# Six of layer 1's forty attention units multiplied as three f16 products instead of one f32 product

## The chip, the core and the metric

One core of a Trainium2 chip runs the whole layer as one program. The metric is the device time of one execution in microseconds (us). The numbers of the kernel before are the median of three timed runs and one profiled execution. The engines in the profile are PE (TensorE matmuls; PEld is its weight loads), DVE (VectorE), ACT (ScalarE), POOL (GpSimd) and SP (SyncE), which here only issues DMAs.

## The reference

The layer takes 1250 nodes with 768 features and 41,250 edges. It adds three things to the nodes: a graph network with two attention layers, a linear attention, and a mixture of 8 experts. The change lies in the first attention layer of the graph network, which has 4 heads of 192 features:

```
h = (x @ W).reshape(n, H, C)
s_src = (h * a_src).sum(-1)
s_dst = (h * a_dst).sum(-1)
e = jax.nn.leaky_relu(s_src[src] + s_dst[dst], NEG_SLOPE)
emax = jax.ops.segment_max(e, dst, num_segments=n)
ee = jnp.exp(e - emax[dst])
denom = jax.ops.segment_sum(ee, dst, num_segments=n)
alpha = ee / denom[dst]
out = jax.ops.segment_sum(alpha[:, :, None] * h[src], dst, num_segments=n)
```

## The kernel before, in words

The kernel does no gather over edges. An early stage counts the edges into a dense table `CT` of 1250 x 1250 (source tiles of 128 nodes on the partitions). Attention is then dense: for one head `h` and one source tile `t` the weights are a matrix of 128 sources by 1250 targets, and the sum over sources is a matmul. One such pair (`h`, `t`) is a **unit**. Layer 1 has 4 heads x 10 tiles = 40 units, unit `10h + t`, in that order on every engine. A unit passes four steps:

- `slopes` (DVE, L1611): the logits before the exponential, 128 x 1250 f32, from two rows that a DMA copied to all partitions.
- `expo` (ACT, L1189): the exponential, in place.
- `weights` (DVE, L1617): clip and multiply by the edge counts. The result goes to one of three buffers `PT1[unit % 3]`. From unit 3 on it waits until PE has finished unit - 3 (`s_agg`).
- `aggregate` (PE, L2323): ten matmuls, one for each tile of 128 targets. The stationary operand is a 128 x 128 slice of `PT1`, the moving one 193 columns of `G4` (192 features of the head and a column of ones, whose sum is the denominator). They add up in PSUM over the ten units of a head.

DVE's program order in layer 1 is, in iteration i: `slopes(i)`, `weights(i-1)`; in a head's iteration t = 2 also `denominators` of the head before (L1729, waits until PE has finished that head's last unit), and in t = 5 `head_added` (L1736: adds the scaled head to the sum `h2x`). ACT does `expo(i)` and in t = 2, 3, 4 scales the ten result tiles of the head before out of PSUM (`head_scaled`, L1201). PE's unit 10h cannot write its fourth pair of target tiles before ACT has scaled the first pair of the head before.

The features `G` are made some 200 us earlier, in a stage called the G stage here: PE makes `x @ M` for node tile t, ACT scales it out of PSUM to `GBUF` (L1131), DVE reads the two logit columns from it (`logits_out`, L1552), SP stores it to memory (`g_d`, L748). They come back just before layer 1, in three DMAs of tiles 0-1, 2-4 and 5-9. After each of the three, POOL writes the column of ones (L933, L939, L941) and PE waits for that with `s_sel_ready` (9, 10 and 11) in units 0-1, 2-4 and 5-9 of head 0. On SP the third of these DMAs is followed by two stores of rows that are needed later (`xl_d`, L831, semaphore `late_rows`), by the load of the mask, and by the loads of three expert units `held` (L827) into arena memory that is free in layer 1; the expert loads wait for `late_rows`.

Of the kernel before, what the change touches and what calls it, by code (L numbers as in the profile page):

```python
# [5 lines left out]
ALU = mybir.AluOpType  # L6
ACT = mybir.ActivationFunctionType
# [16 lines left out]
def gps_layer(nc, x, src, dst, norm_g, norm_b, W1, a_src1, a_dst1, b1, W2, a_src2, a_dst2, b2, Wu, bu,  # L24
# [27 lines left out]
    with ctx:  # L52
# [22 lines left out]
        def reg(off, words, rows=P):  # L75
            return arena[0:rows, off:off + words]
# [114 lines left out]
        EARLY = 3  # L191
        assert EARLY * NP <= 4608

        def slope_buf(unit):
            return early[:, unit, :] if unit < EARLY else BUF[:, unit % 3, :]

# [134 lines left out]
        rr_d = nc.dram_tensor("rr_d", (H1 * 2 * NT * P,), F32, kind="Internal").ap()  # L331
        fr_d = nc.dram_tensor("fr_d", (2 * NE, P, 2, UNIT), F16, kind="Internal").ap()

        held = range(0, 3)
        graphed = range(3, 5)
        masked = range(6, 9)
        summed = (5, 9, 10, 11)
        freed = (14,)
        late = (12, 13, 15)
        assert sorted([*held, *graphed, *masked, *summed, *freed, *late]) == list(range(2 * NE))  # L340
        NCONV = 2 * NE * NPIECE

        def piece(c):
# [211 lines left out]
        sums_out = (s_sum0_out, s_sum1_out)  # L555
        brows_in = (s_brow0_in, s_brow1_in)
        z_in = rows_back + brows_in
        assert NT % 2 == 0
        XAS = 8 * NT
        masks_in = (s_mask0_in, s_mask1_in)  # L560
# [78 lines left out]
        def _(sp):  # L639
# [105 lines left out]
            conv_in(NKV + 2)  # L745
            for t in range(NT):
                sp.wait_ge(s_g_copied, t + 1)
                sp.dma_start(g_d[:, t * GW:(t + 1) * GW], GBUF[:, t % 3, :]).then_inc(gbufs[t % 3], 16)  # L748
                if t:
                    convs(conv_of_g[t - 1])  # L750
                if t == 1:
                    sp.wait_ge(s_kvsum_ready, 1)
                    sp.dma_start(brow, bu.partition_broadcast(P)).then_inc(s_bias_in, 16)
                if t == 8:
                    sp.wait_ge(s_stage_low, 3 * CUTS)
                    weight(3, Wu[0:D, :])
# [83 lines left out]
                rr_load(h)  # L840
            sp.wait_ge(s_agg, agg_done(H1 * NT))
            sp.dma_start(LXT.rearrange("p b r k n -> p (b r k n)"), xl_d.bitcast(F16)).then_inc(late_rows, 16)
            sp.wait_ge(s_head_out, 5 * H1)
            sp.wait_ge(s_late_psum, 2 * len(LATER))
            for u in graphed:
# [26 lines left out]
        def _(pool):  # L872
# [56 lines left out]
            for r in (0, 2 * KC, 4 * KC):  # L929
                select(g.affine_select(out=rows_of, in_=rows_of, compare_op=ALU.not_equal, fill=1.0, base=-r,  # L930
                                       pattern=[[-2, KC], [-1, 2], [0, 64]], channel_multiplier=1))
            pool.wait_ge(s_gbuf0, 80)
            select(g.memset(G4[:, 0:2, :, CW], 1.0))  # L933
# [5 lines left out]
            select(g.memset(G4[:, 2:5, :, CW], 1.0))  # L939
            pool.wait_ge(s_gbuf2, 64)  # L940
            select(g.memset(G4[:, 5:NT, :, CW], 1.0))  # L941

            fmade = [0]

# [81 lines left out]
        def _(act):  # L1026
# [97 lines left out]
            for t in range(NT):  # L1124
                act.wait_ge(s_g_psum, t + 1)
                if t >= 3:
                    act.wait_ge(gbufs[t % 3], 16 * (t // 3))
                    act.wait_ge(s_g_ready, t - 2)
                for c in range(2):
                    h = slice(c * 2 * HW, (c + 1) * 2 * HW)  # L1130
                    i = a.activation(GBUF[:, t % 3, h], ps[2 * (t % 2) + c][:, 0:2 * HW], ACT.Identity, scale=rs[:, 3, t:t + 1])  # L1131
# [72 lines left out]

            SCALED = {2: range(0, 4), 3: range(4, 7), 4: range(7, NT)}

            def out_high(n):
                h, a0, a1 = OUT2[n]
                act.wait_ge(s_o2t_psum, 4 + n + 1)
                a.activation(out2T[0:KS, 0, h, a0:a1], PS[0:KS, 2 * 512 + a0:2 * 512 + a1], ACT.Identity, bias=b2c[:, h:h + 1]).then_inc(s_o2t_ready, 1)  # L1210
# [116 lines left out]
        def _(dve):  # L1327
# [220 lines left out]

            def logits_out(t):
                dve.wait_ge(s_g_copied, t + 1)  # L1550
                logits = GBUF[:, t % 3, :].rearrange("p (h n) -> p h n", h=H1)[:, :, CW:CW + 2]
                V.tensor_tensor(ASD[:, :, :, t].rearrange("p r h -> p h r"), logits, bm, ALU.add).then_inc(s_g_ready, 1)  # L1552

            for t in range(NT):
                if t:
                    edges(KV_STEPS + 2 * t)
                    edges(KV_STEPS + 2 * t + 1)
                    logits_out(t - 1)
# [53 lines left out]

            def weights(unit, i, t, deep):
                dve.wait_ge(s_e_ready, unit + 1)
                if i >= deep:
                    dve.wait_ge(s_agg, agg_done(unit + 1 - deep))
                V.scalar_tensor_tensor((PT1 if deep == 3 else PT)[i % deep][:, 0:N], z_of(unit), 2.0, CT[:, t, 0:N], ALU.min, ALU.mult).then_inc(s_p_ready, 1)  # L1617

            dve.wait_ge(s_kvwo_psum, KC)
            for d in range(2):  # L1620
# [135 lines left out]
            def layer1():  # L1756
                for i in range(H1 * NT):
                    h, t = divmod(i, NT)
                    if t == 0 and h:
                        dve.wait_ge(rr_in[h % 2], 16 * (h // 2 + 1))  # L1760
                    if i >= EARLY:
                        slopes(i, h, t)
                    if i >= 2:
                        weights(i - 1, i - 1, (i - 1) % NT, 3)
                    if t == 2 and h:
                        denominators(h - 1)
                    if t == 5 and h:
# [275 lines left out]
        def _(pe):  # L2043
# [152 lines left out]
            for t in range(NT):  # L2196
                if t >= 2:
                    pe.wait_ge(s_g_copied, t - 1)
                for c in range(2):
                    m = product(ps[2 * (t % 2) + c][:, 0:2 * HW], xnt(t * P, (t + 1) * P), cols(MG, c * 2 * HW, (c + 1) * 2 * HW))  # L2200
                    if c:
                        m.then_inc(s_g_psum, 1)
                    edges(KV_STEPS + 2 * t + c)
                if t == 2:
                    pe.wait_ge(s_kvsum_ready, 1)
                    for j in range(KC):
                        m = T.transpose(ps[6 + j // 3][:, (j % 3) * P:(j % 3 + 1) * P], bd[:, j, :], ident[:, :])
# [64 lines left out]
            for n, (c0, w) in enumerate(CH):  # L2272
# [31 lines left out]
                for t in range(t + 2, (c0 + w) // P):  # L2304
# [27 lines left out]
            for i in range(H1 * NT):  # L2332
                h, t = divmod(i, NT)
                if i == NT:
                    pe.wait_ge(s_acc_ready, NT)
                if i < NT:
                    pe.wait_ge(s_sel_ready, 9 if t < 2 else 10 if t < 5 else 11)
                aggregate(i, i, t, h, CW, 3, G4[:, t, h, 0:CW + 1])

            def keep_warm(n, bank):  # L2340
                for _ in range(n):
# [254 lines left out]
```

## Time and profile before

| | us |
|---|---|
| median of 3 runs (lowest, highest) | 963.11 (962.73, 963.61) |
| the profiled execution: its own time | 964.2 |
| its span in the trace | 962.4 |
| PE busy over the span | 912.5 (95%) |
| DVE busy over the span | 746.1 (78%) |
| ACT busy over the span | 350.1 (36%) |
| POOL busy over the span | 134.2 (14%) |

1.8 us of the profiled execution lie outside its span. A row of a timeline gives start and duration of a run of equal instructions; the durations of neighbours overlap, since the next instruction starts before the last one has drained. So the cost of one instruction in a stream is the distance from start to start, called its **pitch** below, and not its duration. An f32 matmul shows as two records, so that a unit of ten matmuls is 20 records. A note in brackets at the end of a row is idle time ahead of it and what ended it.

### The profile page before, as it was taken

How to read it: one execution, taken by the hardware profiler on the slowest of the kernel's cores; microseconds unless marked ns; L12 is line 12 of the kernel's file. 1: busy time of each engine (PE TensorE's matmuls, PEld its weight loads, DVE VectorE, ACT ScalarE, POOL GpSimd, SP SyncE). 2: the span in 40 equal slices, each digit the busy share in tenths (PEclk: the TensorE clock that was granted, in tenths of full speed). 3: DMA queues.
4: the chain of work that ended last, by engine and by line, in shares of the span. 5: the costliest groups of instructions: out<-in, count | busy, mean ns of one | idle time of the engine just before them, and what ended most of it. 6: DMA issues, size and time to landing. Idle time of an engine off the chain costs nothing.

```text
span 962.4 us, 17237 instructions
## 1 busy us (share of the span) xinstructions
PE 912.5 (95%) x6379; PEld 670.4 (70%) x6381; DVE 746.1 (78%) x1704; ACT 350.1 (36%) x464; POOL 134.2 (14%) x153
## 2 busy tenths in 40 slices
PE   6899999989999999999999999989997899999995
PEld 5667676756665555567799999679866666666662
DVE  7878999997877799895889997889989544444443
ACT  5751212122235314314345552465446223232320
POOL 3400000000002000000000000020010344545441
PEclk9999999999999999999999999999998899999998
DMA  9610212246367689697792000189475668778860
GB/s 324 193 60 24 77 62 70 72 172 236 116 215 226 215 270 267 186 285 259 246 390 83 12 1 1 34 196 330 167 283 216 258 162 196 185 183 195 201 156 3
DMA packets 78844, 164.29 MB, mean 171 GB/s; under 512 B 28308, under 2 KB 47638, under 8 KB 75818
## 3 DMA queue, kind: packets, MB, share of 16 engines
q1 hardware_dynamic: 63402, 117.18, 35.9%
q0 software_dynamic: 10944, 38.22, 16.5%
q10 hardware_dynamic: 4416, 7.78, 2.2%
q8 instruction: 54, 0.88, 0.4%
q14 instruction: 28, 0.23, 0.1%
HBM read 109.13 MB, written 50.51 MB: 166 GB/s over the span
## 4 chain that ended last, share of the span: by engine, by line
PE 72%; DVE 18%; DMA 3%; issue 3%; ACT 2%; SPq 1%; DVEq 1%; ACTq 0%; POOLq 0%; POOL 0%
PE PS L2050 46%; PE PS L2323 15%; PE PS L2151 3%; DVE arena L1784 3%; PE PS L2521 2%; DVE arena L1611 1%; DVE arena L1432 1%; DVE arena L1617 1%; DMA arena<-in_L_ffn_W_dram 1%; PE PS L2162 1%; PE PS L2536 1%; PE PS L2342 1%; DVE arena L1594 1%; DVE arena L1497 1%; PE PS L2219 1%
## 5 line engine op out<-in xcount | busy, mean ns | idle before, releaser
L2050 PE MATMUL PS<-arena 128*128 128x384 f16 (+7 forms) x3396 | 561.5, 321 | 7.8 <-DVE arena L2040 3.0
L2050 PEld LDWEIGHTS PS<-arena 128*128 128x128 f16 (+2 forms) x3396 | 319.9, 99 | 214.3 <-issue 10.0
L2323 PE MATMUL PS<-arena 128*128 128x193 f32 (+1 forms) x1200 | 178.4, 310 | 3.2 <-DVE arena L1617 2.5
L2323 PEld LDWEIGHTS PS<-arena 128*128 128x128 f32 x1200 | 176.4, 191 | 5.3 <-DVE arena L1617 3.8
L1189 ACT ACTIVATE arena<-arena,AS 128x1250 f32<-128x1250 f32 x60 | 79.9, 1338 | 74.7 <-DVE arena L1611 74.6
L1617 DVE SCALAR_TENSOR_TENSOR arena<-arena 128x1250 f32<-128x1250 f32 x60 | 87.1, 1453 | 5.8 <-PE PS L2323 5.7
L1497 DVE TENSOR_SCALAR arena<-arena 128x240 f16<-128x240 f16 x324 | 88.8, 274 | 0.0
L1611 DVE SCALAR_TENSOR_TENSOR arena<-arena,AS 128x1250 f32<-128x1250 f32 x55 | 83.0, 1508 | 0.0
L1496 DVE TENSOR_SCALAR arena<-arena 128x128 f16<-128x128 f16 x324 | 79.8, 246 | 0.1
L2039 DVE SCALAR_TENSOR_TENSOR arena<-PS,arena 128x768 f32<-128x768 f32 x27 | 25.8, 957 | 62.6 <-PE PS L2050 62.6
L1321 ACT ACTIVATE arena<-PS 128x1536 f16<-128x1536 f16 x27 | 39.1, 1449 | 74.8 <-PE PS L2521 74.8
L1594 DVE CUSTOM_DVE_ANT_0 arena<-arena 128x1250 bf16<-128x1250 f32 x40 | 58.3, 1457 | 0.8
L1004 POOL DMA_INDIRECT out_dram<-arena x27 | 43.3, 1602 | 87.8 <-DVE arena L2040 58.0
L1070 ACT ACTIVATE arena<-arena 128x768 f16<-128x768 f32 x48 | 39.8, 838 | 32.0 <-DMA arena<-in_L_ffn_W_dram 32.0
L1437 DVE SCALAR_TENSOR_TENSOR arena<-arena 128x768 f16<-128x768 f32 x48 | 45.9, 966 | 4.1 <-ACT arena L1070 3.8
L1489 DVE TENSOR_TENSOR arena<-arena,PS 128x240 f32 x81 | 32.3, 399 | 19.0 <-PE PS L2151 14.4
L1099 ACT ACTIVATE arena<-arena 128x768 f32<-128x768 f32 x10 | 8.3, 843 | 100.1 <-DVE arena L1446 100.1
L2151 PE MATMUL PS<-arena 128*128 128x240 f16 x324 | 42.4, 266 | 2.5 <-DVE arena L1489 2.5
L2017 DVE SCALAR_TENSOR_TENSOR arena<-PS,arena 128x384 f32<-128x384 f32 x27 | 15.0, 557 | 37.9 <-PE PS L2050 36.1
L2151 PEld LDWEIGHTS PS<-arena 128*128 128x128 f16 x324 | 31.4, 98 | 11.2 <-DVE arena L1497 3.1
L1315 ACT ACTIVATE arena<-arena 128x384 f32<-128x384 f32 x27 | 14.1, 522 | 68.6 <-DVE arena L2017 68.6
L987 POOL DMA_INDIRECT arena<-xf_d,arena x27 | 26.0, 963 | 62.7 <-DVE arena L1992 54.7
(276 smaller groups left out, 914.0 us busy)
## 6 DMA issues: line engine op xcount, KB each, us to landing
arena<-in_L_ffn_W_dram SPq DMA_DIRECT2D x48, 384.0 KB, 3.8
fr_d<-arena SPq DMA_DIRECT2D x48, 384.0 KB, 3.3
arena<-fr_d SPq DMA_DIRECT2D x16, 1152.0 KB, 12.3
arena<-in_x_dram SPq DMA_DIRECT2D x18, 384.0 KB, 5.6
arena<-rr_d SPq DMA_DIRECT2D x4, 1280.0 KB, 8.6
g_d<-arena SPq DMA_DIRECT2D x10, 388.0 KB, 2.4
acc_d<-arena SPq DMA_DIRECT2D x10, 384.0 KB, 3.4
xf_d<-arena ACTq DMA_DIRECT2D x10, 384.0 KB, 3.5
```

The costliest lines, as they stand in the source:

```text
L1004: g.indirect_dma_start(out=out, out_offset=bass.IndirectOffsetOnAxis(ap=found[:, i:i + 1].bitcast(U32), axis=0), in_=Yb[:, i % 2, :], in_o ...
L1070: a.activation(cbuf[b][:, PIECE:PIECE + PIECE // 2].bitcast(F16), cbuf[b][:, 0:PIECE], ACT.Copy, scale=UP).then_inc(s_conv_high, 1)
L1189: a.activation(z, z, ACT.Exp, bias=AS2[:, h, t:t + 1]).then_inc(s_e_ready, 1)
L1437: V.scalar_tensor_tensor(buf[:, 0:PIECE // 2].bitcast(F16), buf[:, 0:PIECE], UP, buf[:, PIECE:PIECE + PIECE // 2].bitcast(F16), ALU.mult, ...
L1496: V.tensor_scalar(ohlo[:, u % OB, j, :], iota[:, 0:P], kc[:, 1, j, u:u + 1], None, ALU.is_equal)
L1497: i = V.tensor_scalar(ohk[:, u % OB, j, :], iota[:, 0:NT * W], kc[:, 0, j, u:u + 1], None, ALU.is_equal)
L1594: V.tensor_tensor_reduce(out=junk1[:, 0:N], in0=arow1[h][:, 0:N], in1=mask1[d % 2].rearrange("p t d -> p (t d)")[:, 0:N], scale=1.0, scala ...
L1611: V.scalar_tensor_tensor(z_of(unit), RR[:, h % 2, 0, 0:N], AS8[:, h, t:t + 1], RR[:, h % 2, 1, 0:N], ALU.add, ALU.max).then_inc(s_t2_ready, 1)
L1617: V.scalar_tensor_tensor((PT1 if deep == 3 else PT)[i % deep][:, 0:N], z_of(unit), 2.0, CT[:, t, 0:N], ALU.min, ALU.mult).then_inc(s_p_rea ...
L2050: m = T.matmul(out, left[i][x], right[i][y], start=first and i + r == 0, stop=last and 3 * i + r == n - 1)
L2151: i = T.matmul(ps[4 + u % 2][:, 0:NT * W], ohlo[:, u % OB, j, :], ohk[:, u % OB, j, :], start=j == 0, stop=j == EJ - 1)
L2323: m = T.matmul(ps[sum_bank(h, b)][:, r * (C + 1):(r + 1) * (C + 1)], (PT1 if deep == 3 else PT)[i % deep][:, d * P:(d + 1) * P], feats, st ...
```

## The change

The units of `SPLIT` = 8, 13, 18, 23, 28, 33 (tiles 3 and 8 only) are multiplied in another form. Their weights and their features are each held as an f16 high part and an f16 low part (the rest). Then high x high, high x low and low x high are added: 30 f16 matmuls stand where 10 f32 matmuls stood. For that

- ACT makes the high part of the weights (`weights_high`) and DVE the low part (`weights_low`), into a ring of two pairs in the arena memory where expert unit 2 was held; that unit's load moves behind layer 1 (`paired`);
- in the G stage, tiles 3 and 8 are written in parts: ACT writes the high part, DVE the low part (`logits_out`), SP and PE wait for DVE there;
- POOL writes the column of ones head by head for these tiles (1 in the high part, 0 in the low part), and also pads the pairs' columns 1250 to 1279, for which it waits for `late_rows`;
- `weights` of unit u + 3 waits for `weights_low(u)` where it waited for PE's unit u.

```diff
+        SPLIT = (8, 13, 18, 23, 28, 33)
+        SPLIT_TILES = sorted({u % NT for u in SPLIT})
+        pairs = reg(2 * UNIT, 2 * NP).bitcast(F16).rearrange("p (b r n) -> p b r n", b=2, r=2)
...
+        def runs(t, c):
+            h = 2 * c
+            kinds = [k * NT + t in SPLIT for k in (h, h + 1)]
+            return [(h, h + 2, kinds[0])] if kinds[0] == kinds[1] else [(h, h + 1, kinds[0]), (h + 1, h + 2, kinds[1])]
...
-        held = range(0, 3)
+        held = range(0, 2)
+        paired = (2,)
...
             for t in range(NT):
                 sp.wait_ge(s_g_copied, t + 1)
+                if t in SPLIT_TILES:
+                    sp.wait_ge(s_g_ready, t + 1)
                 sp.dma_start(g_d[:, t * GW:(t + 1) * GW], GBUF[:, t % 3, :]).then_inc(gbufs[t % 3], 16)
...
+            for u in paired:
+                experts(u)
...
+            def ones_column(a, b):
+                for t in range(a, b):
+                    for c in range(2):
+                        for h0, h1, split in runs(t, c):
+                            if split:
+                                g.memset(g_pair(G[:, t, :], h0, h1)[:, :, 1, CW], 0.0)
+                                i = g.memset(g_pair(G[:, t, :], h0, h1)[:, :, 0, CW], 1.0)
+                            else:
+                                i = g.memset(G4[:, t, h0:h1, CW], 1.0)
+                return i
...
             pool.wait_ge(s_gbuf2, 64)
-            select(g.memset(G4[:, 5:NT, :, CW], 1.0))
+            pool.wait_ge(late_rows, MASKS + 32)
+            for b in range(2):
+                g.memset(pairs[:, b, 0, N:NP], 1.0)
+                g.memset(pairs[:, b, 1, N:NP], 0.0)
+            select(ones_column(5, NT))
...
+            def weights_high(unit):
+                k = SPLIT.index(unit)
+                if k == 0:
+                    act.wait_ge(s_acc_psum, NT)
+                    act.wait_ge(late_rows, MASKS + 32)
+                if k >= 2:
+                    act.wait_ge(s_agg, agg_done(SPLIT[k - 2] + 1))
+                act.wait_ge(s_p_ready, unit + 1)
+                a.activation(pairs[:, k % 2, 0, 0:N], PT1[unit % 3][:, 0:N], ACT.Copy).then_inc(split_high, 1)
...
                     expo(i, h, t)
+                    if i - 1 in SPLIT:
+                        weights_high(i - 1)
...
             def logits_out(t):
                 dve.wait_ge(s_g_copied, t + 1)
+                if t in SPLIT_TILES:
+                    for c in range(2):
+                        for h0, h1, split in runs(t, c):
+                            if split:
+                                made = v3(ps[2 * (t % 2) + c][:, (h0 - 2 * c) * HW:(h1 - 2 * c) * HW], h1 - h0)
+                                row = g_pair(GBUF[:, t % 3, :], h0, h1)
+                                V.scalar_tensor_tensor(row[:, :, 1, :], made, rs[:, 3, t:t + 1], row[:, :, 0, :], ALU.mult, ALU.subtract)
+                        made = v3(ps[2 * (t % 2) + c][:, 0:2 * HW], 2)[:, :, CW:CW + 2]
+                        i = V.scalar_tensor_tensor(ASD[:, :, 2 * c:2 * c + 2, t].rearrange("p r h -> p h r"), made, rs[:, 3, t:t + 1],
+                                                   bm[:, 2 * c:2 * c + 2, :], ALU.mult, ALU.add)
+                    i.then_inc(s_g_ready, 1)
+                    return
...
             def weights(unit, i, t, deep):
                 dve.wait_ge(s_e_ready, unit + 1)
-                if i >= deep:
+                if unit - 3 in SPLIT:
+                    dve.wait_ge(split_low, NK + SPLIT.index(unit - 3) + 1)
+                elif i >= deep:
                     dve.wait_ge(s_agg, agg_done(unit + 1 - deep))
...
+            def weights_low(unit):
+                k = SPLIT.index(unit)
+                dve.wait_ge(split_high, NK + k + 1)
+                V.tensor_tensor(pairs[:, k % 2, 1, 0:N], PT1[unit % 3][:, 0:N], pairs[:, k % 2, 0, 0:N], ALU.subtract).then_inc(split_low, 1)
...
                     if i >= 2:
                         weights(i - 1, i - 1, (i - 1) % NT, 3)
+                    if i - 2 in SPLIT:
+                        weights_low(i - 2)
...
+            def aggregate_pairs(unit, t, h):
+                k = SPLIT.index(unit)
+                pe.wait_ge(split_low, NK + k + 1)
+                row = g_pair(G[:, t, :], h, h + 1)
+                for d in range(NT):
+                    b, r = divmod(d, 2)
+                    for x, y in ((0, 0), (0, 1), (1, 0)):
+                        m = T.matmul(ps[sum_bank(h, b)][:, r * (CW + 1):(r + 1) * (CW + 1)], pairs[:, k % 2, x, d * P:(d + 1) * P], row[:, 0, y, 0:CW + 1],
+                                     start=False, stop=False, skip_group_check=True)
+                m.then_inc(s_agg, 1)
```

Two places in the engines' programs show what the diff alone doesn't. The first is POOL just ahead of layer 1, where it writes the ones that PE waits for; `gbuf0` to `gbuf2` are the three DMAs that bring the features back, and `mask0_out` is the semaphore of `late_rows`. Before:

```order
L933 MEMSET arena 128x8 [waits gbuf0,sel_ready]
L936 MEMSET arena 128x30 [waits acc_psum,sel_ready]
L936 MEMSET arena 128x30 x2
L939 MEMSET arena 128x12 [waits gbuf1,sel_ready]
L941 MEMSET arena 128x20 [waits gbuf2,sel_ready]
```

And after, from `gbuf2` on (between `gbuf1` and `gbuf2` there are 9 memsets in place of one):

```order
L974 MEMSET arena 128x30 [waits mask0_out,gbuf2,sel_ready]
L975 MEMSET arena 128x30
L974 MEMSET arena 128x30
L975 MEMSET arena 128x30
L960 MEMSET arena 128x2 x6
L957 MEMSET arena 128x2
L958 MEMSET arena 128x2
L957 MEMSET arena 128x1
L958 MEMSET arena 128x1
L960 MEMSET arena 128x1
L960 MEMSET arena 128x2 x2
```

In place of one memset behind the third DMA there stand 17 behind that DMA and `late_rows`, and only the last of them lets PE start unit 5.

The second place is DVE in head 1, from the wait for head 0's last unit on (L1803 is `denominators`, L1678 `slopes`, L1686 `weights`, L1691 `weights_low`, L1810 `head_added`; `w1t_ready` and `w1t_psum` are the semaphores that the high and the low part use). After:

```order
L1803 RECIPROCAL rden<-PS 128x10 [waits agg]
L1678 SCALAR_TENSOR_TENSOR arena<-arena,AS8 128x1250 [waits p_ready]
L1686 SCALAR_TENSOR_TENSOR arena<-arena 128x1250 [waits agg,e_ready]
L1678 SCALAR_TENSOR_TENSOR arena<-arena,AS8 128x1250 [waits p_ready]
L1686 SCALAR_TENSOR_TENSOR arena<-arena 128x1250 [waits agg,e_ready]
L1678 SCALAR_TENSOR_TENSOR arena<-arena,AS8 128x1250 [waits p_ready]
L1686 SCALAR_TENSOR_TENSOR arena<-arena 128x1250 [waits agg,e_ready]
L1691 TENSOR_TENSOR arena<-arena 128x1250 [waits w1t_ready]
L1810 TENSOR_TENSOR arena<-arena 128x16x96 [waits head_out]
L1810 TENSOR_TENSOR arena<-arena 128x4x96
L1678 SCALAR_TENSOR_TENSOR arena<-arena,AS8 128x1250 [waits p_ready]
L1686 SCALAR_TENSOR_TENSOR arena<-arena 128x1250 [waits w1t_psum,e_ready]
```

Between the wait for head 0's last unit and the low part of unit 13 stand three pairs of `slopes` and `weights`, and `head_added` follows it directly. Before, the same rows stood there without the L1691 row.

## Rows read from the trace of the kernel before

**Rows 1.** Groups of instructions by line, 471 to 603 us, shapes apart.

```profile
L2323 PE MATMUL PS<-arena 128*128 128x193 f32 x800 | 130.9, 327 | 0.6 <-POOL arena L936 0.6
L1611 DVE SCALAR_TENSOR_TENSOR arena<-arena,AS 128x1250 f32<-128x1250 f32 x38 | 57.3, 1508 | 0.0
L1617 DVE SCALAR_TENSOR_TENSOR arena<-arena 128x1250 f32<-128x1250 f32 x39 | 56.7, 1453 | 2.6 <-PE PS L2323 2.5
L1189 ACT ACTIVATE arena<-arena,AS 128x1250 f32<-128x1250 f32 x38 | 50.9, 1339 | 53.9 <-DVE arena L1611 53.8
```

**Rows 2.** Timeline of PE, the start and the end of layer 1.

```profile
471.51 28.66 PE L2323 MATMUL PS<-arena 128*128 128x193 f32 x174 [0.61 <-POOL arena L936]
...
479.75 122.66 PE L2323 MATMUL PS<-arena 128*128 128x193 f32 x750
602.25 0.82 PE L2358 MATMUL PS<-ident,arena 128*96 128x128 f32 x6
```

**Rows 3.** Timeline of DVE at the change from head 0 to head 1.

```profile
504.45 0.22 DVE L1729 RECIPROCAL rden<-PS 128x10 f32<-128x10 f32 x1 [1.74 <-PE PS L2323]
...
507.34 1.51 DVE L1611 SCALAR_TENSOR_TENSOR arena<-arena,AS 128x1250 f32<-128x1250 f32 x1
508.77 1.45 DVE L1617 SCALAR_TENSOR_TENSOR arena<-arena 128x1250 f32<-128x1250 f32 x1
510.14 1.51 DVE L1611 SCALAR_TENSOR_TENSOR arena<-arena,AS 128x1250 f32<-128x1250 f32 x1
...
512.94 2.22 DVE L1736 TENSOR_TENSOR arena<-arena 128x1536 f32<-128x1536 f32 x2
515.08 1.51 DVE L1611 SCALAR_TENSOR_TENSOR arena<-arena,AS 128x1250 f32<-128x1250 f32 x1
```

**Rows 4.** Timeline of PE: f16 matmuls of 240 and 128 columns.

```profile
229.26 0.98 PE L2151 MATMUL PS<-arena 128*128 128x240 f16 x8
230.08 0.82 PE L2207 MATMUL PS<-ident,arena 128*128 128x128 f32 x6
...
719.68 0.83 PE L2455 MATMUL PS<-identh,arena 128*128 128x128 f16 x12 [0.63 <-ACT arena L1295]
720.35 2.57 PE L2050 MATMUL PS<-arena 128*128 128x8 f16 x30
```

**Rows 5.** Groups by line: VectorE and ScalarE operations near the new ones.

```profile
L1940 DVE TENSOR_TENSOR arena<-arena 128x768 f16<-128x768 f32 x10 | 9.5, 950 | 0.0
...
L1451 DVE TENSOR_SCALAR arena<-arena 128x768 f32<-128x768 f32 x10 | 5.5, 552 | 2.5 <-ACT arena L1099 2.5
```

**Rows 6.** Timeline of POOL ahead of and in layer 1.

```profile
471.02 0.23 POOL L936 MEMSET arena<- 128x30 f32 x3 [11.91 <-PE PS L2050]
477.32 0.13 POOL L939 MEMSET arena<- 128x12 f32 x1 [6.07 <-DMA arena<-g_d]
486.52 0.14 POOL L941 MEMSET arena<- 128x20 f32 x1 [9.07 <-DMA arena<-g_d]
```

**Rows 7.** Timeline of SP's DMA issues there.

```profile
478.60 4.55 SPq L831 DMA_DIRECT2D xl_d<-arena  x2
...
488.81 1.32 SPq L827 DMA_DIRECT2D arena<-fr_d  x3
```

**Rows 8.** Timeline of PE around its two idle times of over 2 us.

```profile
637.24 4.13 PE L2389 MATMUL PS<-ident,RC 128*128 128x128 f32 x20 [2.92 <-DVE RC L1792]
...
643.41 2.42 PE L2389 MATMUL PS<-ident,RC 128*128 128x128 f32 x20
...
761.00 0.84 PE L2521 MATMUL PS<-identh,arena 128*128 128x128 f16 x12 [2.14 <-DMA arena<-xf_d,arena]
```

**Rows 9.** Timeline of SP: the load of a weight at the end of the G stage.

```profile
275.25 0.49 SPq L657 DMA_DIRECT2D arena<-in_L_gnn_Wu_dram  x1
```

**Rows 10.** DMA issues, 262 to 300 us: size and time to landing of that load.

```profile
arena<-in_L_gnn_Wu_dram SPq DMA_DIRECT2D x1, 2304.0 KB, 11.7
```

**Rows 11.** Timeline of ACT: the first use of that load.

```profile
288.60 4.23 ACT L1065 ACTIVATE arena<-arena 128x1536 f16<-128x1536 f32 x3
```

More of the change, by code:

```diff
@@ L192, in gps_layer, with g_pair @@
         assert EARLY * NP <= 4608
+        SPLIT = (8, 13, 18, 23, 28, 33)
+        SPLIT_TILES = sorted({u % NT for u in SPLIT})
+        pairs = reg(2 * UNIT, 2 * NP).bitcast(F16).rearrange("p (b r n) -> p b r n", b=2, r=2)
+        assert 2 * UNIT + 2 * NP <= KC * NP and SPLIT[0] >= 5 and SPLIT[-1] < (H1 - 1) * NT + 8
+        def runs(t, c):
+            h = 2 * c
+            kinds = [k * NT + t in SPLIT for k in (h, h + 1)]
+            return [(h, h + 2, kinds[0])] if kinds[0] == kinds[1] else [(h, h + 1, kinds[0]), (h + 1, h + 2, kinds[1])]
+        def g_pair(row, h0, h1):
+            return row[:, h0 * HW:h1 * HW].bitcast(F16).rearrange("p (h r n) -> p h r n", h=h1 - h0, r=2)
         def slope_buf(unit):
@@ L339, in gps_layer @@
         late = (12, 13, 15)
-        assert sorted([*held, *graphed, *masked, *summed, *freed, *late]) == list(range(2 * NE))
+        assert sorted([*held, *paired, *graphed, *masked, *summed, *freed, *late]) == list(range(2 * NE))
         NCONV = 2 * NE * NPIECE
@@ L557, in gps_layer @@
         z_in = rows_back + brows_in
+        split_high = s_w1t_ready
+        split_low = s_w1t_psum
         assert NT % 2 == 0
@@ L931, in _ @@
                                        pattern=[[-2, KC], [-1, 2], [0, 64]], channel_multiplier=1))
+            def ones_column(a, b):
[8 more added lines that the diff above has]
+                return i
             pool.wait_ge(s_gbuf0, 80)
-            select(g.memset(G4[:, 0:2, :, CW], 1.0))
+            select(ones_column(0, 2))
             pool.wait_ge(s_acc_psum, NT)
@@ L938, in _ @@
             pool.wait_ge(s_gbuf1, 64)
-            select(g.memset(G4[:, 2:5, :, CW], 1.0))
+            select(ones_column(2, 5))
             pool.wait_ge(s_gbuf2, 64)
-            select(g.memset(G4[:, 5:NT, :, CW], 1.0))
+            pool.wait_ge(late_rows, MASKS + 32)
[3 more added lines that the diff above has]
+            select(ones_column(5, NT))
             fmade = [0]
@@ L1129, in _ @@
                 for c in range(2):
-                    h = slice(c * 2 * HW, (c + 1) * 2 * HW)
-                    i = a.activation(GBUF[:, t % 3, h], ps[2 * (t % 2) + c][:, 0:2 * HW], ACT.Identity, scale=rs[:, 3, t:t + 1])
+                    for h0, h1, split in runs(t, c):
+                        made = ps[2 * (t % 2) + c][:, (h0 - 2 * c) * HW:(h1 - 2 * c) * HW]
+                        if split:
+                            to = g_pair(GBUF[:, t % 3, :], h0, h1)[:, :, 0, :]
+                            i = a.activation(to, v3(made, h1 - h0), ACT.Identity, scale=rs[:, 3, t:t + 1])
+                        else:
+                            i = a.activation(GBUF[:, t % 3, h0 * HW:h1 * HW], made, ACT.Identity, scale=rs[:, 3, t:t + 1])
                 i.then_inc(s_g_copied, 1)
@@ L1550, in logits_out @@
                 dve.wait_ge(s_g_copied, t + 1)
+                if t in SPLIT_TILES:
+                    for c in range(2):
+                        for h0, h1, split in runs(t, c):
+                            if split:
+                                made = v3(ps[2 * (t % 2) + c][:, (h0 - 2 * c) * HW:(h1 - 2 * c) * HW], h1 - h0)
[6 more added lines that the diff above has]
+                    return
                 logits = GBUF[:, t % 3, :].rearrange("p (h n) -> p h n", h=H1)[:, :, CW:CW + 2]
@@ L1556, in _ @@
                     edges(KV_STEPS + 2 * t)
+                    if t - 1 in SPLIT_TILES:
+                        logits_out(t - 1)
                     edges(KV_STEPS + 2 * t + 1)
-                    logits_out(t - 1)
+                    if t - 1 not in SPLIT_TILES:
+                        logits_out(t - 1)
                     for c in conv_of_g[t - 1]:
@@ L2198, in _ @@
                     pe.wait_ge(s_g_copied, t - 1)
+                if t - 2 in SPLIT_TILES:
+                    pe.wait_ge(s_g_ready, t - 1)
                 for c in range(2):
@@ L2213, in _ @@
                     pe.wait_ge(s_g_copied, NT)
+                if j == 2 and NT - 2 in SPLIT_TILES:
+                    pe.wait_ge(s_g_ready, NT - 1)
                 if j == 3:
@@ L2337, in _ @@
                     pe.wait_ge(s_sel_ready, 9 if t < 2 else 10 if t < 5 else 11)
-                aggregate(i, i, t, h, CW, 3, G4[:, t, h, 0:CW + 1])
+                if i in SPLIT:
+                    aggregate_pairs(i, t, h)
+                else:
+                    aggregate(i, i, t, h, CW, 3, G4[:, t, h, 0:CW + 1])
             def keep_warm(n, bank):
```

## The prediction

> **What bounds the kernel now.** I read the stage of the forty units first, in the groups by line: PE is busy 130.9 us of it and waited 0.6 us, while DVE's two large operations take 57.3 and 56.7 us [rows 1]. Then the timeline of PE: the 750 records from 479.75 to 602.25 are one row without a gap, so a record has a pitch of 0.1633 us and a unit (20 records) takes 3.27 us [rows 2]. So PE sets the end of layer 1. But the reader should see how close DVE is. `slopes` has a pitch of 508.77 - 507.34 = 1.43, `weights` of 510.14 - 508.77 = 1.37, `head_added` of 515.08 - 512.94 = 2.14 us [rows 3]. A head costs DVE 10 x 2.80 + 2.14 + 0.14 (the reciprocal) = 30.3 us of work, against PE's 32.7. DVE also has to wait once in a head, in iteration t = 2, for PE to finish the head before: 1.74 us at 504.45 [rows 3]. That wait throws away its lead of one unit just ahead of `head_added`. With it DVE is at 32.0 of 32.7 us. The ring of three buffers is DVE's only reserve.
>
> **PE's part of the change.** An f16 matmul of 240 columns has a pitch of (230.08 - 229.26)/8 = 0.1025 us, one of 128 columns of (720.35 - 719.68)/12 = 0.056 us, each with a weight load of its own [rows 4]. On the line between them 193 columns take 0.056 + 65 x (0.0465/112) = 0.083 us. A split unit takes 30 x 0.083 = 2.49 in place of 3.27 us: 0.78 less, and 4.7 us less over the six. This is the gain on offer. Bounds for the pitch are the two rows themselves, but the operation is so near the line that I keep 0.080 to 0.090. The Trainium skill ("TensorE: Matmul & The Clock Gate", Back-to-back issue gap) speaks against the gain: it says that in a stream of weight loads and matmuls the spacing is about 81 ns at 128 columns. The trace has 56 ns there, so the rule doesn't hold here; by an estimate from the page (some 89 ns at 193 columns) a split unit would take 2.7 us and the total below would be 0.8 us higher.
>
> **DVE's part.** `weights_low` is a subtraction of an f16 tensor from an f32 one into f16, 128 x 1250. The nearest row is the same form at 768 columns, 0.950 us [rows 5]; `weights` with 1250 has 1.453 [rows 1], and between them a column costs 1.04 ns, so the new operation takes 1.45 us, and 1.37 of pitch like `weights`. Bound below: an operation with one tensor input takes 0.552 us for 768 columns [rows 5], which would make 0.72 here; I see nothing that gives this to two inputs. In exchange nothing leaves DVE.
>
> Now the walk. Let T be the time when PE ends unit 10h - 1. PE's end reaches DVE 0.33 us later: 504.45 against the end of unit 9 at 471.51 + 10 x 3.267 = 504.18, and the small semaphore and drain times at other waits are alike [rows 2, 3]. DVE then has the reciprocal, three pairs and the low part of unit 10h + 3: 0.33 + 0.14 + 3 x 2.80 + 1.37 = 10.24, ready for PE at T + 10.4. PE is through units 10h to 10h + 2 at T + 9.8 and waits **0.6 us**. The next low part (unit 10h + 8) comes after `head_added` and five pairs: 10.24 + 2.14 + 14.0 + 1.37 = 27.75, ready at T + 27.9. PE ends unit 10h + 7 at 10.4 + 2.49 + 4 x 3.27 = 25.95 and waits **1.95 us**. It ends unit 10h + 9 at 27.9 + 2.49 + 3.27 = T + 33.7. DVE reaches its wait of the next head at 27.75 + 5.6 = 33.35, just before, so the pattern repeats. A head with two split units takes 33.7 in place of 32.7 us: **+1.0 us** each, for heads 1 and 2.
>
> Head 0 has unit 8 alone and neither the reciprocal nor `head_added`, so DVE has full lead: -0.78. Head 3 has unit 33, a wait of 0.6 and a gain of 0.78; behind it no low part follows and DVE's pairs (2.80) are shorter than PE's units (3.27), so it catches up: -0.2. Sum over the layer, POOL left aside: 2 x 1.0 - 0.78 - 0.2 = **+1.0 us**. The other way round: 4.7 gained, 3 x 0.6 + 2 x 1.95 = 5.7 given back.
>
> **ACT's part.** `weights_high` is 1.34 us like `expo` [rows 1]. ACT idled 53.9 us in the stage [rows 1] and gets 6 x 1.34 = 8.0 more. DVE asks for the high part only after a pair of its own, 2.8 us after ACT could begin, so the idle time hides it: 0. Without that cover it would be up to 1.34 us for each split unit.
>
> **POOL's part.** PE needs `s_sel_ready` 11 for unit 5. It starts that unit at 471.51 + 5 x 3.267 = 487.85 [rows 2]. Before, POOL's one memset for it was done at 486.66 [rows 6], 1.2 us early. Now POOL waits for `late_rows` too. The second of those stores is issued behind the first from 478.60 to 483.15, and SP, which waits for the same semaphore value ahead of the expert loads, goes on at 488.81 [rows 7]. From there POOL has 17 memsets. Three in a row take 0.23 us with 0.12 for one [rows 6], so a pitch of 0.055: 16 x 0.055 + 0.12 = 1.0 us. With the semaphores PE starts unit 5 at about 489.95: a wait of **2.1 us**. It isn't absorbed: DVE is ahead at that time and only waits longer, then goes into the walk above with the same T-relative times. Bounds: at 0.137 us for each memset [rows 6] the ones of units 5 to 9 come at 491.2, and those of units 2 to 4 (9 memsets from 477.32) 0.5 us after PE wants them: together +3.4. From below: if `late_rows` came no later than the third feature load, 0.
>
> **The G stage.** DVE's low parts for tiles 3 and 8 are 582 columns in two instructions, plus two small ones: under 1.3 us for each tile by the 768-column row [rows 5]. PE needs them two tiles (some 7 us) later, so this is hidden. SP's store of tile 8 waits for them, and behind it on SP stands the load of Wu, issued at 275.25 and landed 11.7 us later at 286.95 [rows 9, 10]; ACT takes it at 288.60 [rows 11]. I put the delay at 1.8 us (ACT's third instruction and DVE's turn), so it lands at 288.75: +0.1, counted as 0. If DVE's turn is a microsecond later, PE pays about 1 us in the next stage. The moved expert load has an idle DMA queue behind layer 1: 0.
>
> **Sum.** +1.0 + 2.1 = +3.1 us. The profiled execution would go from 964.2 to 967.3. It stands 1.1 us above the median of the runs, so the median goes from 963.1 to **966.2 us**.
>
> **Rivals.** What a measurement of this kernel can tell from no change is about 0.2%, 1.9 us.
>
> - *POOL's wait costs nothing* (`late_rows` lands as early as the features, since both are in flight together): +1.0 us, 964.1. Against it is SP's row at 488.81, which waits for the same value. Chance 0.16.
> - *The stall slows PE's clock, or Wu comes late.* After an idle time of 2.92 us twenty f32 matmuls took 4.13 instead of 2.42 us; after one of 2.14 us the next group ran at full rate [rows 8]. A stall of 2.1 us lies just on the safe side. If the memsets make it 2.9, layer 1 pays 0.8 + 1.7 more: 968.7. Late Wu gives 967.2. Chance 0.18 together.
> - *The low part is cheap* (the other side). All of it hangs on the price p of L1691. With POOL's wait, the walk gives +3.1 at p = 1.37, 0 at 0.7, and -2.1 at 0.2, where the two waits at units 18 and 28 nearly vanish. So it is faster below 0.7 us and visibly faster only below 0.25. At 0.7 the time is 963.1, at 0.2 it is 961.0. For it speaks that its output and one input are 16 bits wide; against it the 768-column row of the very same form. Chance 0.08.
> - *The forecast*, both stalls as above: 965.2 to 967.2. Chance 0.58.
>
> **The range.** 964.0 reaches down to the case without POOL's wait and leaves out the cheap low part; 968.4 takes in a late Wu, memsets near their bound and the most of a clock drop. Chances: the forecast and the second rival are slower by over 0.2% (0.58 + 0.18, less 0.02 for its lower edge): 0.74. Within it: POOL's rival 0.16, a part of the cheap low part 0.03 and that edge, rounded to 0.20. Faster: 0.06.
>
> **What would show it.** Split units of 30 records 83 ns apart; L1691 at 1.45 us each; PE waiting for POOL ahead of unit 5 for about 2 us, with POOL's 17 memsets starting at about 488.8; PE waiting for DVE about 0.6 us ahead of units 13, 23, 33 and 1.95 us ahead of 18 and 28; layer 1 ending at about 605.4 instead of 602.25. I am wrong if L1691 is well under 1.3 us, if POOL starts its memsets before 487, or if the granted clock falls behind the stall.

## The result, and the profile after

| | before | after |
|---|---|---|
| median (lowest, highest) | 963.29 us, 11 runs (962.12, 966.82) | 965.61 us, 11 runs (963.66, 969.47) |
| the profiled execution's span | 962.4 us | 964.3 us |
| PE busy over the span | 912.5 us | 911.7 us |
| DVE busy over the span | 746.1 us | 756.3 us |

The ratio of the times is 1.0026, with a 95% interval of 1.0015 to 1.0037: the changed kernel is slower, by 1.4 to 3.6 us. That is more than the 0.2% which the prediction called visible in its best estimate, but the interval reaches down below it. 966.2 us was forecast, with a range of 964.0 to 968.4. The kernel before was timed once more, beside the kernel apart from the layer that is told of below, and took 959.81 us in a single run, 3.5 us below its median here. Single runs on different occasions can thus differ by more than the change; only the two sets of eleven are compared.

Read the page after first. PE has less work than before, DVE ten microseconds more, and the time rose. In the chain that ended last, PE had 72% and DVE 18% before:

```profile
PE 911.7 (95%) x6441; PEld 667.1 (69%) x6441; DVE 756.3 (78%) x1716; ACT 357.4 (37%) x472; POOL 133.6 (14%) x180
...
PE 65%; DVE 22%; issue 5%; DMA 4%; ACT 2%; SPq 1%; DVEq 1%; POOLq 0%; ACTq 0%; POOL 0%
```

So work left the engine that set the end and came back as waits for another. The groups by line of the stage, 455 to 610 us, shapes apart, say which (L2414 is `aggregate`, L2399 `aggregate_pairs`, L1691 `weights_low`, L1255 `weights_high`, L960 and L967 POOL's memsets). They answer to [rows 1]:

```profile
L2414 PE MATMUL PS<-arena 128*128 128x193 f32 x680 | 112.7, 327 | 2.2 <-POOL arena L960 1.6 <-POOL arena L967 0.6
...
L1686 DVE SCALAR_TENSOR_TENSOR arena<-arena 128x1250 f32<-128x1250 f32 x40 | 58.1, 1452 | 1.9 <-ACT arena L1229 1.4 <-PE PS L2414 0.4
...
L2399 PE MATMUL PS<-arena 128*128 128x193 f16 x180 | 16.1, 246 | 4.2 <-DVE arena L1691 4.2
...
L1691 DVE TENSOR_TENSOR arena<-arena 128x1250 f16<-128x1250 f32 x6 | 8.7, 1452 | 0.0
L1255 ACT ACTIVATE arena<-arena 128x1250 f16<-128x1250 f32 x6 | 7.5, 1247 | 2.3 <-DVE arena L1686 1.9
```

`weights` waited 2.5 us for PE before [rows 1]. Now its row names 1.4 us for ACT and 0.4 for PE, both in head 0. (The 1.4 lie ahead of 492.50, where `weights` of unit 8 also has to wait for PE's unit 5. PE ends that unit at 488.86 + 3.27 = 492.13, by the timeline below, so I read this wait as one for the late unit 5 and not for ACT.) DVE's room shows better in the waits of its reciprocals at the change of heads, 465 to 604 us before and to 606 after (in all, times, longest):

```profile
DVE rden L1729 <- PE PS L2323: 5.2, 3, 1.7
```

```profile
DVE rden L1803 <- PE PS L2414: 1.5, 3, 0.6
```

Most of that room is gone. PE waited 0.6 us in the whole stage and now waits 0.6 + 1.6 us for POOL and 4.2 us for the low parts.

The timeline of PE is the view to work with (start, duration, and idle time ahead in brackets). It answers to [rows 2]:

```profile
470.65 16.57 PE L2414 MATMUL PS<-arena 128*128 128x193 f32 x100 [0.61 <-POOL arena L967]
488.86 10.07 PE L2414 MATMUL PS<-arena 128*128 128x193 f32 x60 [1.63 <-POOL arena L960]
498.76 2.68 PE L2399 MATMUL PS<-arena 128*128 128x193 f16 x30
501.28 13.26 PE L2414 MATMUL PS<-arena 128*128 128x193 f32 x80
514.77 2.69 PE L2399 MATMUL PS<-arena 128*128 128x193 f16 x30 [0.23 <-DVE arena L1691]
517.30 13.26 PE L2414 MATMUL PS<-arena 128*128 128x193 f32 x80
532.29 2.69 PE L2399 MATMUL PS<-arena 128*128 128x193 f16 x30 [1.73 <-DVE arena L1691]
534.82 13.26 PE L2414 MATMUL PS<-arena 128*128 128x193 f32 x80
548.37 2.69 PE L2399 MATMUL PS<-arena 128*128 128x193 f16 x30 [0.30 <-DVE arena L1691]
550.90 13.26 PE L2414 MATMUL PS<-arena 128*128 128x193 f32 x80
565.89 2.69 PE L2399 MATMUL PS<-arena 128*128 128x193 f16 x30 [1.73 <-DVE arena L1691]
568.42 13.26 PE L2414 MATMUL PS<-arena 128*128 128x193 f32 x80
581.92 2.69 PE L2399 MATMUL PS<-arena 128*128 128x193 f16 x30 [0.24 <-DVE arena L1691]
584.45 19.79 PE L2414 MATMUL PS<-arena 128*128 128x193 f32 x120
604.08 0.82 PE L2452 MATMUL PS<-ident,arena 128*96 128x128 f32 x6
```

The change within layer 1 can be added up from these fifteen rows. A record of the f32 units has the pitch of 0.1633 us of [rows 2], so 100 of them fill 16.33 us, 80 fill 13.07 and 60 fill 9.80. What lies beyond that up to the next start is a wait, in the measure of pitches (the bracket is smaller, since it counts from the modelled end of the last matmul, which has to drain):

| piece, from starts | us |
|---|---|
| unit 5: 488.86 - 470.65 - 16.33 | +1.88 |
| unit 8: 498.76 - 488.86 - 9.80 | +0.10 |
| units 13, 23, 33: 514.77 - 501.28 - 13.07, and so on | +0.42, +0.48, +0.43 |
| units 18, 28: 532.29 - 517.30 - 13.07, and so on | +1.92, +1.92 |
| six units of 2.52 to 2.53 us in place of 3.27 | -4.43 |
| sum | +2.72 |

Layer 1 took 602.25 - 471.51 = 130.74 us before [rows 2] and takes 604.08 - 470.65 = 133.43 now: +2.69. The table closes to 0.03 us. It has to, nearly, since its pieces cut the layer up without a gap: it shows where the time lies. What each wait is for is read from its releaser and from DVE's and POOL's rows.

Behind layer 1 the rest of the program is equally long in both traces (962.4 - 602.25 = 360.15 us before, 964.3 - 604.08 = 360.22 after). Ahead of it, layer 1 begins 0.86 us earlier in the trace after. The lead is there at 208.10 us already, where the first matmul of the G stage starts, against 209.07 before, and the program up to there isn't changed. From 26 to 100 us, PE's mean granted clock is 1.00 in the trace after and 0.98 in that of before. So I take the lead for a difference between executions and not for the change; with one trace of each that is an argument and not shown. It accounts for the span: +2.69 - 0.86 = +1.8, against 964.3 - 962.4 = 1.9.

### The profile page after: what moved, and what is told of

Its sections match the earlier page's. It is cut to its first block, busy times and chain, and to the rows that moved or that the text cites. A ratio compares the mean times of both kernels' runs of the same rounds, so it can differ in the third digit from the quotient of the medians.

```text
span 964.3 us, 17414 instructions
## 1 busy us (share of the span) xinstructions
PE 911.7 (95%) x6441; PEld 667.1 (69%) x6441; DVE 756.3 (78%) x1716; ACT 357.4 (37%) x472; POOL 133.6 (14%) x180
## 4 chain that ended last, share of the span: by engine, by line
PE 65%; DVE 22%; issue 5%; DMA 4%; ACT 2%; SPq 1%; DVEq 1%; POOLq 0%; ACTq 0%; POOL 0%
PE PS L2126 46%; PE PS L2414 6%; DVE arena L1686 4%; DVE arena L1678 4%; PE PS L2227 3%; PE PS L2615 2%; DVE arena L1484 1%; DMA arena<-in_L_ffn_W_dram 1%; PE PS L2238 1%; PE PS L2399 1%; DMA xl_d<-arena 1%; PE PS L2630 1%; DVE arena L1661 1%; DVE arena L1549 1%; PE PS L2299 1%
## 5 line engine op out<-in xcount | busy, mean ns | idle before, releaser
L2414 PE MATMUL PS<-arena 128*128 128x193 f32 (+1 forms) x1080 | 160.3, 309 | 6.0 <-DVE arena L1686 3.6
L2414 PEld LDWEIGHTS PS<-arena 128*128 128x128 f32 x1080 | 156.5, 191 | 8.6 <-DVE arena L1686 3.8
L1686 DVE SCALAR_TENSOR_TENSOR arena<-arena 128x1250 f32<-128x1250 f32 x60 | 87.1, 1453 | 4.9 <-PE PS L2414 2.5
L1678 DVE SCALAR_TENSOR_TENSOR arena<-arena,AS 128x1250 f32<-128x1250 f32 x55 | 83.0, 1509 | 0.0
```

The source lines that it names most:

```text
L1678: V.scalar_tensor_tensor(z_of(unit), RR[:, h % 2, 0, 0:N], AS8[:, h, t:t + 1], RR[:, h % 2, 1, 0:N], ALU.add, ALU.max).then_inc(s_t2_ready, 1)
L2414: m = T.matmul(ps[sum_bank(h, b)][:, r * (C + 1):(r + 1) * (C + 1)], (PT1 if deep == 3 else PT)[i % deep][:, d * P:(d + 1) * P], feats, st ...
```

## The experiments

One kernel apart from the layer was run on the chip. The cause in the layer itself was tested by no run that undoes a part of the change; what stands for that is the accounting above and a comparison within the trace, and the last part of this section says what was left open.

**m2_ops_alone: the new operations by themselves.** Two prices carry the forecast and stood in no row of before: the low part on DVE (1.37 us a piece by the forecast, 0.7 and less by the rival that ends on the other side) and 193-column f16 matmuls with a weight load each. A third price says whether POOL could make the low part instead. The kernel's core, in which `W`, `R` and `Z` are f32 and `Hi`, `Lo`, `LoP` and `Mv` f16:

```diff
+            i = V.tensor_tensor(Z[:, 0:1250], W[:, 0:1250], Hi[:, 0:1250], ALU.subtract)
...
+            V.tensor_tensor(Lo[:, 0:1250], W[:, 0:1250], Hi[:, 0:1250], ALU.subtract).then_inc(s_a, 1)
+            dve.wait_ge(s_b, 2)
+            for k in range(8):
+                dve.wait_ge(s_a, 2 + k)
+                V.scalar_tensor_tensor(Z[:, 0:1250], R[:, 0:1250], 2.0, W[:, 0:1250], ALU.min, ALU.mult).then_inc(s_a, 1)
...
+            pool.wait_ge(s_b, 2)
+            pool.wait_ge(s_a, 3)
+            g.tensor_tensor(LoP[:, 0:1250], W[:, 0:1250], Hi[:, 0:1250], ALU.subtract).then_inc(s_b, 1)
...
+            for _ in range(8):
+                for k in range(30):
+                    i = nc.tensor.matmul(PS[:, 0:193], Hi[:, (k % 10) * P:(k % 10 + 1) * P], Mv[:, 0:193], start=k == 0, stop=k == 29)
```

POOL makes its subtraction twice alone, ahead of DVE's eight operations, and a third time when the first of the eight is done.

What was expected:

> A small kernel apart from the layer (its output is a copy of x, nothing of the reference is computed): the new operations by themselves. DVE's f16 = f32 - f16 over 128 x 1250 alone: 1.45 us if it runs at one column a cycle (theory), about 0.8 us if 16-bit operands speed it up (the rival of the cheap low part). PE's stream of f16 matmuls of 193 columns with a weight load each: 83 ns start to start at the granted clock of 1.0. The same subtraction on POOL, alone and beside a DVE operation with two f32 inputs: no number from the traces but 0.86 and 1.43 us for 384 f32 columns; 2.8 to 4.7 us are expected for 1250.

Its span was 31.8 us. The timeline of DVE and POOL (L74 writes the difference as f32, L77 as f16; L88, L90 and L93 are POOL's, L81 DVE's eight operations in the form of `weights`):

```profile
9.03 1.45 DVE L74 TENSOR_TENSOR Z<-W,Hi 128x1250 f32<-128x1250 f32 x1
10.52 1.46 DVE L77 TENSOR_TENSOR Lo<-W,Hi 128x1250 f16<-128x1250 f32 x1
12.13 2.56 POOL L88 TENSOR_TENSOR LoP<-W,Hi 128x1250 f16<-128x1250 f32 x1 [11.69 <-DVE Lo L77]
14.76 2.56 POOL L90 TENSOR_TENSOR LoP<-W,Hi 128x1250 f16<-128x1250 f32 x1
17.35 14.17 DVE L81 SCALAR_TENSOR_TENSOR Z<-R,W 128x1250 f32<-128x1250 f32 x8 [5.38 <-POOL LoP L90]
18.96 3.77 POOL L93 TENSOR_TENSOR LoP<-W,Hi 128x1250 f16<-128x1250 f32 x1 [1.64 <-DVE Z L81]
```

and of PE, in a window from 16 to 28 us:

```profile
15.80 12.41 PE L105 MATMUL PS<-Mv,Hi 128*128 128x193 f16 x147
```

The low part costs what `weights` costs, 1.46 us, and the width of its output changes nothing (1.45 with an f32 output). The rival of a cheap low part falls (its chance was 0.08), and the size that the trace after shows for it (1.452 us mean) is the operation's own and not a contention of the layer. The matmul: 147 of them span 12.41 us with a last duration of 0.26, so the pitch is (12.41 - 0.26)/146 = 0.083 us, as on the line that the prediction drew between 128 and 240 columns. That holds for the even part of the stream. At its beginning it is slower: the view by windows counts 14 and 19 matmuls in the 2 us from 8 and from 10 us, against 27 in each 2 us from 12 to 28, at a granted clock of 1.00 in all of them. All 240 took 22.05 us. No run shows why; in the layer the split units have the pitch of the even part.

On POOL the same subtraction takes 2.56 us alone, which is below the 2.8 to 4.7 that were expected, and 3.77 us with DVE at work beside it. The reader should look at what it does to DVE. The eight operations of L81, by their line (shortest, median and longest duration in ns, then first and last start), and the two of them that lie between 20 and 24 us:

```profile
L81 DVE SCALAR_TENSOR_TENSOR Z<-R,W x8: 1460/1461/3700, 17.4 to 30.1; 128x1250 f32<-128x1250 f32 x8
...
18.85 5.20 DVE L81 SCALAR_TENSOR_TENSOR Z<-R,W 128x1250 f32<-128x1250 f32 x2
```

Their median is 1461 ns and one took 3700. Eight at the median would make 8 x 1.46 = 11.7 us and a few gaps between; the group's 14.17 is longer by about that one's excess. The long one is the third: the second starts at 18.85 and ends 1.46 us later at 20.31, and the third runs to 18.85 + 5.20 = 24.05, from 20.35 on. POOL's operation runs from 18.96 to 22.73. These times fit two operations that took turns. Of POOL's 3.77 us, 1.35 lie beside the second operation of DVE, which kept its 1.46; the other 2.42 are about POOL's 2.56 alone. Of the third's 3.70, 2.38 lie beside POOL, and the 1.32 behind POOL's end are nearly its own 1.46. That is an estimate from one execution, in which POOL's span is rough.

So DVE lost 3.70 - 1.46 = 2.24 us by one operation of POOL, where making the low part itself costs it 1.37. By that number, moving the low part to POOL in this form (two SBUF inputs on each engine) is no way out; in the layer it wasn't tried. The Trainium skill ("GPSIMD Engine Reference", Specifications) says that POOL's access to SBUF is shared with VectorE and contended by DVE instructions with two SBUF inputs; the rows agree with that, and they give a size.

**What the trace itself compares.** The walk behind the forecast says that one more DVE operation costs PE nothing where DVE has a full lead, and a wait where `denominators` or `head_added` has eaten that lead. The trace has both cases. DVE at units 8 and 13:

```profile
492.50 1.46 DVE L1686 SCALAR_TENSOR_TENSOR arena<-arena 128x1250 f32<-128x1250 f32 x1 [1.45 <-ACT arena L1229]
...
495.76 1.46 DVE L1686 SCALAR_TENSOR_TENSOR arena<-arena 128x1250 f32<-128x1250 f32 x1 [0.38 <-PE PS L2414]
497.14 1.46 DVE L1691 TENSOR_TENSOR arena<-arena 128x1250 f16<-128x1250 f32 x1
...
504.77 0.22 DVE L1803 RECIPROCAL rden<-PS 128x10 f32<-128x10 f32 x1 [0.57 <-PE PS L2414]
504.91 1.46 DVE L1678 SCALAR_TENSOR_TENSOR arena<-arena,AS 128x1250 f32<-128x1250 f32 x1
...
511.89 1.45 DVE L1686 SCALAR_TENSOR_TENSOR arena<-arena 128x1250 f32<-128x1250 f32 x1
513.26 1.45 DVE L1691 TENSOR_TENSOR arena<-arena 128x1250 f16<-128x1250 f32 x1
514.64 2.21 DVE L1810 TENSOR_TENSOR arena<-arena 128x1536 f32<-128x1536 f32 x2
...
530.79 1.44 DVE L1691 TENSOR_TENSOR arena<-arena 128x1250 f16<-128x1250 f32 x1
```

At unit 8 DVE is so far ahead that it has to wait for a buffer (0.38 us at 495.76). Its low part ends at 497.14 + 1.46 = 498.60, PE takes the unit at 498.76, and PE's own work would have brought it there at 498.66: nearly the whole gain of 0.74 us is kept. At unit 13 DVE starts behind its wait for head 0's last unit. From 504.91 to 513.26 it does three pairs without a pause and its low part ends at 514.71, 0.06 us before PE starts the unit at 514.77. At unit 18 it is `head_added` (514.64 to 516.77) and five pairs, and the low part ends at 532.23, again 0.06 before PE's start at 532.29. The three operations are the same; only DVE's lead differs. That is a comparison inside one execution, and it doesn't separate the low part from everything else that a split unit brings (the longer chain over ACT, above all). Against that chain as the cause speaks that DVE never waited for a high part: no idle time stands ahead of L1691.

**What was not tried.** These versions would undo one part each. None of them has a measured time; the numbers are worked out from the rows and are estimates.

- *POOL's ones ahead of its wait.* The four pads move behind the ones of tiles 5 to 9, and the first split unit waits for the pads as well (that wait on PE isn't in the lines below):

```diff
             pool.wait_ge(s_gbuf2, 64)
+            select(ones_column(5, NT))
             pool.wait_ge(late_rows, MASKS + 32)
             for b in range(2):
                 g.memset(pairs[:, b, 0, N:NP], 1.0)
-                g.memset(pairs[:, b, 1, N:NP], 0.0)
-            select(ones_column(5, NT))
+                i = g.memset(pairs[:, b, 1, N:NP], 0.0)
+            select(i)
```

  Unit 5's wait should go, 1.9 us, and the layer come to about +0.8 us. That is still no gain, and too little to be told from no change. The rival is that DVE's later waits shrink or grow in its place.
- *The low part on 64 of 1250 columns*, which leaves out most of it: the waits of units 13 to 33 should vanish, and layer 1 be 2.5 us shorter than before.
- *The kernel before with POOL's wait alone*: +1.9 us expected.
- *Split units only where DVE has its lead*, or one in each head (8, 18, 28) instead of two. The walk gives these 1 to 2 us less than before with POOL's order mended. It is the version to run next.

## Why the prediction was right

Each of its steps can be set against a row. The two stalls came where it said, in nearly the sizes that it gave.

- **PE's gain.** Forecast: 30 x 0.083 = 2.49 us a unit, 4.7 us in all. Measured: 2.52 to 2.53 and 4.43, from 2.52 to 2.53 in place of 3.27. The pitch is right; some 0.03 us at the change of form was left out. By the estimate from the Trainium skill ("TensorE: Matmul & The Clock Gate", Back-to-back issue gap) a split unit would have taken 2.7 us, and the rows contradict it.
- **DVE's low part.** Forecast 1.45 us and 1.37 of pitch. Measured 1.452, and 498.51 - 497.14 = 1.37. (The lower bound of 0.72 beside it is a pitch, drawn from a duration of 0.552; in proportion to the columns alone that row would give 0.90. The forecast doesn't use it.)
- **The walk.** Forecast waits of 0.6 us at units 13, 23 and 33 and 1.95 at 18 and 28, 5.7 us in all. Measured 0.42, 0.48, 0.43 and 1.92, 1.92: 5.17. The mis-sized term is mainly the delay from PE's end to DVE, taken as 0.33 us. The prediction's own two numbers, 504.45 and 504.18, give 0.27. In the trace after, unit 9 ends at 501.28 + 3.27 = 504.55 by pitches, and the reciprocal starts at 504.77, 0.22 later. That shortens only the first wait in a head, since the second is from one low part to the next. Heads 1 and 2 were to take 33.7 us each: from unit 9's end at 504.55 to unit 19's at 534.82 + 3.27 = 538.09 it is 33.54.
- **"32.0 of 32.7".** This reading of how full DVE is was wrong, though the forecast doesn't rest on it. It adds DVE's wait of 1.74 us to its work of 30.3 as if the wait were a fixed cost. The wait is room: behind the low parts it is 0.57 us at 504.77 and 1.5 for all three heads, where it was 5.2. The same sum with two low parts would make a head 32.0 + 2.7 = 34.7 us long; the walk said 33.7, and 33.54 was measured. The work by itself says more: with two low parts it is 30.3 + 2.7 = 33.0 us on DVE, against 32.7 - 1.5 = 31.2 on PE. So DVE sets the length of such a head, and 33.54 is its work and the wait that is left.
- **POOL's wait.** Forecast 2.1 us, measured 1.88. POOL's timeline answers to [rows 6]:

```profile
488.11 0.12 POOL L974 MEMSET arena<- 128x30 f16 x1 [11.12 <-DMA xl_d<-arena]
...
488.32 0.26 POOL L960 MEMSET arena<- 128x2 f32 x6
...
488.63 0.17 POOL L960 MEMSET arena<- 128x1 f32 x3
```

  It names the releaser, `xl_d`, whose two stores are `late_rows`. SP, which waits for the same value, goes on beside it, as before [rows 7]:

```profile
477.90 4.38 SPq L849 DMA_DIRECT2D xl_d<-arena  x2
...
487.99 0.85 SPq L845 DMA_DIRECT2D arena<-fr_d  x2
```

  The second of the stores is issued at 478.51 and lands 9.46 us later, at 487.97. The mis-sized term is the 17 memsets: from 488.11 to 488.80 they take 0.69 us and not 1.0, since those of 1 or 2 columns follow each other faster (six in 0.26 us) than the 30-column ones (0.05 from start to start), and from 30-column ones the pitch came. The rival in which this wait costs nothing falls.
- **The clock.** The prediction had the stall "just on the safe side". In layer 1 it was: three windows of the trace after, with the granted clock behind POOL's column (busy times with counts of PE, PEld, DVE, ACT, POOL, then clock, DMA share, GB/s):

```profile
484.00:490.00 6.00, 4.37 (x27) 4.07 (x26) 6.00 (x6) 2.69 (x3) 0.70 (x17) 1.00 1.13 319
490.00:500.00 10.00, 10.00 (x70) 9.91 (x69) 8.18 (x7) 3.81 (x3) 0.00 (x0) 1.00 0.98 416
500.00:605.00 105.00, 100.66 (x694) 98.88 (x691) 98.27 (x86) 54.66 (x65) 0.00 (x0) 1.00 0.08 29
```

  It stays at its upper level, 2.4 GHz, behind the 1.63 us of idle time and behind the two of 1.73.

  But it fell soon behind layer 1, which no step foresaw. This is the window from 612 to 624 us after, and one row of six matmul records in it; below them the same six before:

```profile
612.00:624.00 12.00, 12.00 (x48) 7.16 (x48) 11.96 (x23) 2.55 (x2) 0.00 (x0) 0.72 0.01 1
...
612.45 4.09 PE L2470 MATMUL PS<-arena,a2c 96*128 96x512 f32 x6
```

```profile
610.62 2.40 PE L2376 MATMUL PS<-arena,a2c 96*128 96x512 f32 x6
```

  In the windows of 1 us from 613 to 616 and from 620 to 622 the clock is 0.50, its lower level of 1.2 GHz. Before, it was 1.00 in this stretch. PE had no idle time over 0.45 us between 604 and 612, so the prediction's picture, that a fall comes behind an idle time of 2.9 us, doesn't cover this one. Whether the change has a part in it, one trace of each can't say. It cost nothing: DVE, busy 11.96 of these 12 us, sets the pace there, and goes from its first maximum of layer 2 to the next `slopes` in 638.92 - 609.61 = 29.31 us, against 637.10 - 607.78 = 29.32 before. The prediction names a fall of the clock behind the stall as a sign of being wrong. This one is not behind the stall, and that it met a stretch in which DVE sets the pace is luck. (The "twenty f32 matmuls" of that passage are ten, in twenty records.)
- **ACT and the G stage.** ACT's high part took 1.25 us and no wait on PE names it. In the G stage PE took 279.06 - 208.10 = 70.96 us against 70.83, and Wu, which SP now issues at 275.92 against 275.25 [rows 9] in an execution that is 0.9 us ahead, is taken by ACT earlier than before, not later. Measured against the 0.9 us of lead, the issue is some 1.5 us late, where 1.8 were forecast. The load took 9.5 us to land and not 11.7; even with 11.7 it would have been there at 287.62, just ahead of ACT. It answers to [rows 11]:

```profile
287.76 4.23 ACT L1100 ACTIVATE arena<-arena 128x1536 f16<-128x1536 f32 x3
```

  The forecast of 0.1, counted as 0, holds, and the rival of a late Wu falls.

The sum was +3.1 us and layer 1 came out at +2.69. That is 0.4 less: 0.2 from POOL, 0.5 from the waits, and 0.3 back from the smaller gain. The errors are small, and that they partly cancel is luck. The medians differ by 965.61 - 963.29 = 2.3 us, and the interval of 1.4 to 3.6 holds both sums. The forecast time itself, 966.2, stood on a median of before of 963.1 from three runs.

What the runs leave open: the two causes, POOL's order and DVE's low part, are read from releasers and closed by addition, in one execution. Their strongest support is that the waits were forecast one by one before the trace was seen. That undoing one gives its share back was only argued.

## What to carry to other kernels

A kernel at 95% of one engine can have a second one close behind it, and the share of busy time over the whole program (78% here) doesn't show that. Add up each engine's work over one period of the loop, before the change and with it. Here DVE had 30.3 us and PE 32.7 in a head, and with two split units 33.0 and 31.2. Then find the point where its program order makes it wait for the first engine, and walk from there to each result that the first engine needs. Don't count the wait itself as a cost, since it shrinks when work is added. Here the walk reached the low part of unit 10h + 3 some 10.2 us behind the wait, where PE was through its work in 9.8. So an operation of 1.37 us which saved PE 0.74 us lost the trade over a head, and kept it only at the one unit where DVE was waiting for a buffer. And a preparation that nobody needs yet, put ahead of a signal that somebody does need, inherits the later event: the pads for unit 8 made unit 5 wait 1.88 us for a store.

## What the runs showed of the hardware

- One subtraction of 128 x 1250 on POOL, in one execution: a DVE operation of two SBUF inputs that was running when it began kept its 1.46 us, the next took 3.70, and POOL's own took 3.77 instead of 2.56. The times fit engines that take turns for whole operations. DVE lost more (2.24 us) than the operation would have cost it.
- Memsets of one or two columns on POOL follow each other within 0.02 to 0.04 us, though each has a duration of 0.10 to 0.11.
- A subtraction into f16 from an f32 and an f16 input takes 1.46 us for 1250 columns, the same as into f32 (1.45): nothing is won by a narrow output in this form.
- PE's granted clock fell to its lower level twice for some 3 us (613 to 616, 620 to 622) with no idle time over 0.45 us in the 8 us ahead, and stayed at its upper level behind idle times of 1.63 and 1.73 us. Six matmul records of 512 columns took 4.09 us in the fall, against 2.40.
